# Row-indexed writes of a token scatter: bursts of four on four semaphores, against one by one on two

## What is computed

```
xn = layernorm(x)
s  = causal attention(xn)                       # 2 query heads, one shared key and value, RoPE
probs = softmax(xn @ router_w.T)                # 8 experts
out   = sum over the 2 best experts e of a token:
          p_e * (((gelu(xn @ wg_e.T + bg_e)) * (xn @ w1_e.T + b1_e)) @ w2_e.T + b2_e)
x  = x + s * silu(out)
xn = layernorm(x)
s  = conv, decayed running sums, linear memory and a gated feed-forward on xn
g  = silu(tanh(xn @ (w @ aux1 @ aux2) + bias))
x  = x + s * g
```

## Time and profile before

| | us |
|---|---|
| median of 3 runs | 528.92 |
| profiled execution, whole | 530.34 |
| its span on the core | 528.5 |
| TensorE (PE) busy, share of the span | 515.4, 98% |
| VectorE (DVE) busy | 389.8, 74% |
| ScalarE (ACT) busy | 314.4, 59% |
| GpSimd (POOL) busy | 235.1, 44% |
| the 64 row-indexed writes of line 601, busy on GpSimd | 64.0 |
| GpSimd idle just before them | 35.9 |

### The profile page before, as it was taken

The page is one execution under the profiler, slowest core; times in us unless marked ns, Lnnn a source line. Parts: engine busy times, 40 slices in busy tenths (PEclk is TensorE's granted clock), DMA queues, the critical chain, the costliest instruction groups (busy, mean ns, idle before and its releaser), DMA issues. The chain is left out here.

```text
span 528.5 us, 12881 instructions
## 1 busy us (share of the span) xinstructions
PE 515.4 (98%) x3193; PEld 387.5 (73%) x3194; DVE 389.8 (74%) x1106; ACT 314.4 (59%) x830; POOL 235.1 (44%) x245
## 2 busy tenths in 40 slices
PE   9999999999999999999999999998999999999997
PEld 5756667677779999999999999976445545554544
DVE  6659778977886777767776777757788888788654
ACT  5635555555657666666666666657776657656511
POOL 4434766666631333333333333344476647523310
PEclk9999999999999999999999999999999999999999
DMA  7930133335528656556565655519100000000001
GB/s 233 371 118 7 42 98 104 105 106 162 148 69 105 166 132 157 140 149 146 147 151 144 150 145 151 127 34 286 27 0 20 1 20 22 20 0 22 20 12 30
DMA packets 85268, 54.01 MB, mean 102 GB/s; under 512 B 53088, under 2 KB 70016, under 8 KB 85104
## 3 DMA queue, kind: packets, MB, share of 16 engines
q1 hardware_dynamic: 80912, 44.66, 33.6%
q0 software_dynamic: 4320, 8.92, 4.6%
HBM read 37.82 MB, written 15.74 MB: 101 GB/s over the span
## 5 line engine op out<-in xcount | busy, mean ns | idle before, releaser
L1894 ACT ACTIVATE AR<-bank,BGT 128x128 f32<-128x128 f32 x284 | 81.3, 369 | 69.4 <-PE bank L928 69.4
L637 POOL DMA_INDIRECT rows_y<-YO,W1E x71 | 69.0, 972 | 118.0 <-DVE YO L1408 115.0
L1425 DVE SCALAR_TENSOR_TENSOR AR<-bank,B1T,AR 128x128 f32<-128x128 f32 x284 | 80.1, 344 | 3.4 <-ACT AR L1894 2.1
L601 POOL DMA_INDIRECT slots_x<-XR,SLOT x64 | 64.0, 1000 | 35.9 <-DMA slots_x<-XR,SLOT 19.5
L946 PE MATMUL bank<-W2E,AR 128*128 x568 | 75.1, 275 | 0.5 <-DVE AR L1425 0.5
L928 PE MATMUL bank<-AR,WGE 128*128 128x128 f32 x568 | 75.1, 275 | 0.0
L937 PE MATMUL bank<-AR,WGE 128*128 128x128 f32 x568 | 75.0, 275 | 0.0
L946 PEld LDWEIGHTS bank<-W2E,AR 128*128 128x128 f32 x568 | 69.1, 192 | 0.7 <-issue 0.7
L937 PEld LDWEIGHTS bank<-AR,WGE 128*128 128x128 f32 x568 | 69.1, 192 | 0.0
L928 PEld LDWEIGHTS bank<-AR,WGE 128*128 128x128 f32 x568 | 69.1, 192 | 0.0
L1799 ACT ACTIVATE AR<-bank,AR 128x512 f32<-128x512 f32 (+1 forms) x64 | 33.8, 528 | 53.2 <-DVE AR L1330 53.1
(11 more groups left out here) (216 smaller groups left out, 912.5 us busy)
## 6 DMA issues: line engine op xcount, KB each, us to landing
WGE<-in_wgu SPq DMA_DIRECT2D x71, 256.0 KB
XG<-slots_x SPq DMA_DIRECT2D x140, 32.0 KB
slots_x<-W1E SPq DMA_DIRECT2D x7, 585.0 KB, 8.5
X<-in_x SPq DMA_DIRECT2D x8, 256.0 KB, 5.8
SPARE<-in_wgu SPq DMA_DIRECT2D x8, 256.0 KB
W2E<-in_w SPq DMA_DIRECT2D x8, 256.0 KB
XR<-rows_y SPq DMA_DIRECT2D x8, 256.0 KB, 4.8
XNT<-rows_y SPq DMA_DIRECT2D x8, 256.0 KB, 5.3
```

The costliest lines, as they stand in the source:

```text
L601: pool.indirect_dma_start(out=slots_x, out_offset=bass.IndirectOffsetOnAxis(ap=SLOT[:, k, n:n + 1], axis=0), in_=XR[:, n, :], in_offset=No ...
L637: pool.indirect_dma_start(out=rows_y, out_offset=bass.IndirectOffsetOnAxis(ap=DST[:, j:j + 1], axis=0), in_=YO[q % 2][:], in_offset=None). ...
L1425: s = dve.scalar_tensor_tensor(out=HT[u][:, c, :], in0=B[3 + u][:, c * P:(c + 1) * P], scalar=B1T[:, bass.ds(e, 1), c], in1=ZB[u][:, c, :] ...
L1894: act.activation(ZB[u][:, c, :], B[1 + u][:, c * P:(c + 1) * P], ACT.Gelu, bias=BGT[:, bass.ds(e, 1), c]).then_inc(c_gelu, 1)
```

## The change

`SCAT_BURST` is gone. The tags still go by groups of 4 tiles (`GROUP = 4`), but the writes use two semaphores in turn (`IN_FLIGHT = 2`): write n waits until all earlier writes on its own semaphore have landed, the last of which is write n - 2. `second_tags` gets waits for both semaphores, for the landing of the writes whose tags it replaces. The waits for the end (SyncE before `load_tiles`, GpSimd before line 628) count on two semaphores and not on four. The number, size, order and data of the writes are the same.

```diff
-SCAT_BURST = 4
+GROUP = 4
+
+IN_FLIGHT = 2
...
-        scat = [sem(f"scat{i}") for i in range(SCAT_BURST)]
+        scat = [sem(f"scat{i}") for i in range(IN_FLIGHT)]
...
-            for i in range(SCAT_BURST):
-                sp.wait_ge(scat[i], 16 * 2 * NT // SCAT_BURST)
+            for i in range(IN_FLIGHT):
+                sp.wait_ge(scat[i], 16 * 2 * NT // IN_FLIGHT)
...
             def send_rows(k, group, burst):
 
-                for i in range(SCAT_BURST):
-                    n = group * SCAT_BURST + i
-                    if burst and i == 0:
-                        for j in range(SCAT_BURST - 1):
-                            pool.wait_ge(scat[j], 16 * burst)
-                    if burst and i == SCAT_BURST - 1:
-                        pool.wait_ge(scat[i], 16 * burst)
+                for i in range(GROUP):
+                    n = group * GROUP + i
+                    place, before = i % IN_FLIGHT, (burst * GROUP + i) // IN_FLIGHT
+                    if before > 0:
+                        pool.wait_ge(scat[place], 16 * before)
                     pool.indirect_dma_start(
                         out=slots_x, out_offset=bass.IndirectOffsetOnAxis(ap=SLOT[:, k, n:n + 1], axis=0),
-                        in_=XR[:, n, :], in_offset=None).then_inc(scat[i], 16)
-
-            def second_tags(group):
-
-                tiles = slice(group * SCAT_BURST, (group + 1) * SCAT_BURST)
+                        in_=XR[:, n, :], in_offset=None).then_inc(scat[place], 16)
+
+            def second_tags(group, sent_before):
+
+                tiles = slice(group * GROUP, (group + 1) * GROUP)
+                for place in range(IN_FLIGHT):
+                    pool.wait_ge(scat[place], 16 * (sent_before + GROUP) // IN_FLIGHT)
                 pool.tensor_copy(XR[:, tiles, P:], TAG[:, 1, tiles, :]).then_inc(tagged, 1)
...
                 send_rows(0, group + 1, 2 * group + 1)
-                second_tags(group)
+                second_tags(group, 2 * group * GROUP)
...
                 send_rows(1, group, 2 * group + 2)
-                second_tags(group + 1)
+                second_tags(group + 1, (2 * group + 1) * GROUP)
```

More of the change, by code:

```diff
@@ L592, in send_rows @@
             def send_rows(k, group, burst):
-                for i in range(SCAT_BURST):
-                    n = group * SCAT_BURST + i
-                    if burst and i == 0:
-                        for j in range(SCAT_BURST - 1):
-                            pool.wait_ge(scat[j], 16 * burst)
-                    if burst and i == SCAT_BURST - 1:
-                        pool.wait_ge(scat[i], 16 * burst)
+                for i in range(GROUP):
[3 more added lines that the diff above has]
+                        pool.wait_ge(scat[place], 16 * before)
                     pool.indirect_dma_start(
                         out=slots_x, out_offset=bass.IndirectOffsetOnAxis(ap=SLOT[:, k, n:n + 1], axis=0),
-                        in_=XR[:, n, :], in_offset=None).then_inc(scat[i], 16)
-            def second_tags(group):
-                tiles = slice(group * SCAT_BURST, (group + 1) * SCAT_BURST)
+                        in_=XR[:, n, :], in_offset=None).then_inc(scat[place], 16)
[3 more added lines that the diff above has]
+                    pool.wait_ge(scat[place], 16 * (sent_before + GROUP) // IN_FLIGHT)
                 pool.tensor_copy(XR[:, tiles, P:], TAG[:, 1, tiles, :]).then_inc(tagged, 1)
             pool.wait_ge(tagged, 1)
-            for group in range(0, NT // SCAT_BURST, 2):
+            for group in range(0, NT // GROUP, 2):
                 send_rows(0, group, 2 * group)
@@ L620, in _ @@
                 send_rows(1, group, 2 * group + 2)
-                second_tags(group + 1)
+                second_tags(group + 1, (2 * group + 1) * GROUP)
                 pool.wait_ge(tagged, group + 3)
                 send_rows(1, group + 1, 2 * group + 3)
-            for i in range(SCAT_BURST):
-                pool.wait_ge(scat[i], 16 * 2 * NT // SCAT_BURST)
+            for i in range(IN_FLIGHT):
+                pool.wait_ge(scat[i], 16 * 2 * NT // IN_FLIGHT)
             pool.wait_ge(w_c3, 1)
```

## The result

The kernel after takes 538.05 us as the median of 4 runs (537.65 to 539.48), the kernel before 528.81 us beside it: 9.2 us more, a ratio of 1.0169 with a 95% interval of 1.0154 to 1.0184. The forecast was 532.0 us, with a range up to 537.5. The direction and the path of the delay were right, the size was a third of what came, and the time is outside the range. A few executions of any of these kernels, the profiled one of e6 among them, have a low clock early on and take some 8 us longer; the ratios leave them out.

What follows compares the result with a forecast made beforehand. The prediction took TensorE as the bound (busy 515.4 of 528.5 us). The scatter's end moves by 4.6 us, less 1.53 us of slack gives +3.1 us on 528.92, so 532.0 us, range 528.7 to 537.5.

Steps and rivals of the forecast that it cites:

- The slack: Turn to stage 3: the scatter can end 1.53 us later for free; anything beyond delays TensorE in full.
- The stall per pair: Scatter writes: each pair stalls for landing + 0.28 - 2.54 us, summed to 19.3 us against 14.7 before.
- Halfway: Scatter stalls: 19.3 us taken between 14.9 with median landings and 23.7 with the middle of smallest and largest.
- the count with the middle: Scatter stalls summed with the middle between smallest and largest landing of each stretch: 23.7 us, scatter's end +9.0 us.
- The idle time: TensorE before the experts' first matmul: 3.1 us more idle, from a scatter ending 4.6 us later.
- The clock: TensorE behind the gap: rival that half clock adds 1 to 2 us, giving 533.5 us; chance 0.10.
- One wait on a write costs 0.28 us: Scatter writes: a write held by a single wait starts 0.28 us after the landing, as line 637 does.
- The rival of 0.8 us: Scatter writes: each wait costs the full 0.8 us of a group's start; 540 us, up to 548; chance 0.10.
- The tags' waits cost nothing: Copies of tags on GpSimd: the added waits never hold, 0 us taken, at most 4 us for all eight.
- Landings don't shrink with fewer in flight: Scatter writes under weight loads: landings stay long, up to 5.3 us, however few writes are in flight.
- No change: Scatter's end: rival that it moves only +0.2 us, inside the slack, giving 528.9 us; chance 0.17.
- faster: Attention through VectorE: rival that more even writes speed it up, at most 1.00 us, giving 527.9 us; chance 0.04.

Runs made afterwards that it cites:

- e6: The kernel before with its first tile loads held back by two useless GpSimd copies behind the last landing: 529.48 us, ratio 1.0003 to the kernel before.
- e1: The kernel after with four writes in flight in place of two, still one by one: 528.98 us against 529.08 for the kernel before, ratio 1.0002.
- e9: The kernel before with its first tile loads held back by twelve useless GpSimd copies: 538.74 us, ratio 1.021 to the kernel before.
- e7: The kernel before with its first tile loads held back by six useless GpSimd copies: 531.5 us, ratio 1.0046 to the kernel before.
- e3: The kernel after with 22 useless matmuls on TensorE between the attention and the experts' first tile: 536.87 us, ratio 1.0149 to the kernel before.
- e4: The kernel after with the experts' weight loads issued as soon as buffers are free, not paced by TensorE's projections: 534.16 us, ratio 1.0111 to the kernel before.
- e10: The kernel after with one write in flight in place of two: 614.91 us in one run.
- e5: The kernel after without the two waits that the change put into second_tags: 539.36 us, ratio 1.0215 to the kernel before.
- e8: The kernel after with four in flight and ScalarE's last two attention steps swapped: 528.31 us against 528.89 for the kernel before, ratio 0.9989.

## Why the prediction was wrong

**The slack: right as a rule.** A scatter that ends early brings nothing (e1), one that ends late costs one for one plus the clock (e9). As a number, 1.53 us was that of one execution. By the same sum (last write + 2.3 + 4.36 us to the end of the transpose) the untouched writes of e7 and e9 had 5.1 and 2.8 us of slack. The stream of 64 writes, from the first start to the last, is 7.5 us longer after than in the trace before (109.6 against 102.1), but 9 and 11 us longer than in the traces of e9 and e7 (100.8, 98.9). Shift and slack were both read from one late execution, both came out small, and the two errors partly cancelled.

**The stall per pair: right in form, too small in size.** This is the step that failed first: "The median forgets the slow ones and the middle counts them too often; I take 19.3, halfway". Measured are 23.3 us. Two things were wrong with the sum. It has one landing for each pair, but either write of a pair can be held: in the kernel after 11.3 us of the stalls stand before the first writes of the pairs and 12.0 before the second. And its rows were thin: the trace of the kernel before gives a landing for only 16 of its 64 writes, the third of each group, one to three for each stretch of the earlier trace rows. Halfway had no reason of its own; it happens to be near what the mean of the 16 landings gives (2.9 us, 31 x 0.65 = 20 us). That the count with the middle gave 23.7 is luck in part: it charged 6.1 us to the stretch from 139 to 147, where the kernel after has 3.0, and less than was measured to the two stretches from 85 to 118. With 23.7 us the scatter's end would have come out at 154.4 + 9.0 = 163.4 us, the idle time at 7.5 us and the time at 536.4 us, still without the clock.

The end lay at 161.2 us in the traces of the kernel after and of e3 (last writes at 158.89 and 158.90), 2.2 us beyond the 159.0 of the forecast and not the full 4.0 us: the stream began 0.75 us earlier (49.30, before 50.05), and its other pauses and the writes' own work were 1.1 us shorter together.

**The idle time: 3.1 us forecast, 5.5 us measured.** 1.9 us come from the first tile's transpose, which started at 164.96 and not at 158.45 + 4.6 = 163.05. The other 0.5 us are TensorE, which reached the turn earlier: 159.41 for its last weighted values, not 159.88. The 530.34 us beside a median of 528.92 said that something in the traced execution was late, and the earlier trace rows had it; I carried the difference to the end of the sum, where it doesn't belong, since the gap is measured from where TensorE really arrives.

**The clock: a rival at 0.10 that came true.** The sum had the clock at nothing, and this is the second step that failed. The rival put it at 1 to 2 us; it is 2.2 us in the kernel after, and e3 shows that the gap is its cause. Taking it away brought 1.2 us in the medians. Treating it as a case beside the forecast was a mistake of its own: it isn't another mechanism but the consequence of the same gap, so its chance had to grow with the size of the gap, and the upper end of the range (7.5 us of idle time) should have carried it in full. 528.92 + 7.5 + 2 = 538.4 would have held the result. The Trainium skill has this: "TensorE: Matmul & The Clock Gate", section "Why this matters for your kernels", lists as a rule that TensorE should have no long idle gaps between bursts of matmuls, lest its throughput drop. The trace agrees, with 1.2 GHz behind a gap of 5.33 us and 2.4 GHz behind the 22 matmuls of e3.

**One wait on a write costs 0.28 us: right.** e4 has the quiet stream at 1.28 us, e10 one write in 2.55 us. The rival of 0.8 us (chance 0.10) is out. But it is what a write pays behind a copy of the tags: there a wait for the copy stands beside the one for the landing, and in e10, looked at up to 180 us, these writes (74.54, 89.01, 127.57, 141.06, 175.66) start 0.77 to 0.81 us after the landing, all others 0.2 to 0.3. Both fit a price for the second wait; no run varies their number alone.

**The tags' waits cost nothing: right** as far as e5's spread can tell.

**Landings don't shrink with fewer in flight: right.** With one in flight they still reach 5.2 us, with two in e3 6.0 us, where before it was 5.3. That is the rule of the Trainium skill's page "DMA: Bandwidth & Descriptors" weighed in the prediction, and the trace goes with it: with one in flight there is no other write to delay it, and landings between 70 and 90 us, beside weight loads, still take up to 3.8 us. The delay comes from the loads and not from the other writes.

**No change and faster: out.** Both needed the scatter to end by 155.9 us.

**The balance.** Of the 6.1 us between 3.1 and 9.2, 2.4 are idle time (1.9 for the scatter's end and the loads behind it, 0.5 for TensorE's arrival), 2.2 the clock, 0.5 came later in the kernel, and 1.0 is the early part of the profiled execution, which has nothing to do with the change.

## What to carry to other kernels

The number of writes in flight has to cover the slow landings, not the median one: issue time times the number in flight against the landings under load. Here 2 x 1.27 us lies below many landings beside a weight load, 3 x 1.27 us above nearly all, and the step from two to three is worth 8.5 us while three to four is worth nothing that can be told. The few landings above 5 us didn't matter, since the stream had slack for them.

When a stream off the critical path comes near its deadline, cost three things and not one: the idle time, the clock behind it, and what is queued behind the late transfer. Before that, look at the deadline and the end in more than one execution, or treat their distance as a range.

## What the hardware showed

- GpSimd's 64 writes of 66 KB come 1.27 us apart where nothing holds them. From the first to the last start it is 87 to 88 us with four in flight one by one (e1, e8), against 99 to 102 with the groups of four (before, e7, e9), although both allow four. A group's first write, which waits on three semaphores, starts 0.75 to 0.85 us after the third write's landing in these traces; a write with a single wait starts 0.2 to 0.3 us after it, and one with two waits 0.77 to 0.81 us after it (e10).
- In e4 the clock fell behind a gap of TensorE of 2.38 us; its four runs have mean clocks of 0.983 to 1.000. It also fell behind the gaps of 5.3 us (the kernel after) and 5.6 us (e9), and all eight runs of these two kernels have mean clocks of 0.980 to 0.994.
- A load of 67 x 128 pieces of 8 bytes takes over 7 us to land. A weight load that SyncE issued 1.2 us behind it took 3.6 us on the queue (e3), and 3.7 in e4; one issued 2.1 us behind it took 2.7 (the kernel after).
